# Placing the rows of a mixture of experts: scattered into room per expert, in place of slot lists and gathers

## The chip, the cores and the metric

One of the cores of a Trainium2 chip runs the whole program. The metric is the device time of one execution in microseconds (us). The engines are TensorE (PE in the profile, its weight loads PEld), VectorE (DVE), ScalarE (ACT), GpSimd (POOL) and SyncE (SP). SP and ACT issue plain DMAs; POOL issues the indirect ones, which take their row numbers from a tile in SBUF.

## What is computed

A graph layer of 6250 nodes with 256 features in float32 (100,000 edges), then a mixture of 8 experts, of which each node uses 2. The mixture, cut to what matters:

```python
xt = x.reshape(N, D)                       # 6250 x 256
probs = softmax(xt @ Wr + br)              # 8 experts
top_p, top_idx = top_k(probs, 2)
weights = top_p / top_p.sum(-1, keepdims=True)
xn = (xt - mean) * rsqrt(var + eps)
xe = xn[None] * ln_g[:, None] + ln_b[:, None]
h = gelu(einsum('end,edh->enh', xe, W1) + b1[:, None])     # 256 -> 1024
y = einsum('enh,ehd->end', h, W2) + b2[:, None]            # 1024 -> 256
out = (weights[:, :, None] * take_along_axis(y_tok, top_idx)).sum(1)
x = x + out
```

The kernel computes each expert only for the nodes that chose it, in tiles of 256 (node, choice) pairs.

## The kernel before

NT = 49 tiles of 128 nodes, in G = 7 groups of CT = 7 tiles. P = 128, NP_ = 49 x 128 = 6272 nodes with padding. An expert tile has SLOTS = 256 slots; MT = 56 expert tiles are always computed, which is enough for 12544 pairs wherever they fall. The program has an edge stage (to about 1330 us of the span), a node stage, and the expert stage. All engines run their own instruction stream, written out by hand in order, and meet at semaphores.

**Node stage.** `tensor_nodes`, `vector_nodes`, `scalar_nodes`, `gpsimd_nodes` and `sync_nodes` are one function for each engine. TensorE makes a node tile's last product (second_product, L1452), transposes the node sums (turn, L1461) and multiplies them with the router's weights (logit, L1472), with second_product running 14 tiles ahead. DVE works by group: `scales(g)` writes the normed rows xh (L1588), `measure_rows(g + 2)` adds the products to X (second_sum, L1561) and takes means and variances (L1569 to L1574), `weigh(g - 1)` makes the two weights of each node of the group before (L1623 to L1634), `route(g)` takes logits, the two largest and their indices (L1597 to L1618). ScalarE evicts the transposes (L1767) and takes the exponentials of a group once route has got to s_sm (L1772, L1773). The ring xh has 3 groups; each row is 256 values, 2 weights and 2 expert numbers (DX = 260 words). SP stores X of each group to sum_dram (`summed`) and, once its weights are there, the normed rows to xh_dram in node order (`normed`, L1818).

**After the last group.** DVE compares the chosen experts of all 49 tiles (L1653, L1656), TensorE counts them and ranks them within a tile (L1491, L1492), DVE runs a scan over the tiles for each of the 8 experts (L1662) and makes the table tex of which expert each of the 56 tiles belongs to (L1664 to L1681); this is NODE_EXPERTS, upon which SP begins to load weights. Then each pair has a slot number pos (L1683 to L1695). To turn "node to slot" into "slot to node", for each of the 49 node tiles DVE builds two one-hots from the high and the low part of pos (L1709, L1711), ScalarE scales one by the node number (L1781) and TensorE adds their product up in one PSUM bank (L1499). L1714 to L1722 make of that the slot list slot_i; unused slots point at rows of zeros behind the last node. This is NODE_SLOTS.

**Expert stage.** POOL gathers 128 rows of xh_dram by the slot list, two gathers for each expert tile (`gather`, L2021), two tiles ahead. TensorE transposes them (rows_in, L1881), ScalarE applies the expert's scale and bias (L1983), DVE splits values into a high and a low part (L1924, L1926), TensorE does the up product in three terms (L1896) and the down product (L1909), ScalarE the Gelu between them (L2000). DVE adds the bias and multiplies with the pair's weight (L1965, L1968), and POOL adds the 128 rows into sum_dram by the same slot list (L2039), an indirect DMA with accumulation. SP loads the weights of the tile's expert (`load`, L2043 to L2054). After the last addition sum_dram is copied to the output.

`landed_rows` waits until all normed rows are stored; xh of two groups lies in the region of which the expert stage uses other parts. s_xtra counts the stores of the rows behind the last node.

## Time and profile before

| | us |
|---|---|
| median of 3 timed runs | 2344.48 (2344.31 to 2349.3) |
| the profiled execution | 2321.41 |
| its span, first to last instruction | 2320.0 |

The profile is of one execution. Busy time of each engine over the span, from its page:

| engine | busy us | share |
|---|---|---|
| TensorE, matmuls | 1900.3 | 82% |
| TensorE, weight loads | 1561.9 | 67% |
| DVE | 1658.3 | 71% |
| ScalarE | 1142.4 | 49% |
| POOL | 1279.6 | 55% |

These shares are means over stages with different limits, so the rows below are read by stretch. Other views used: the chain of work that ended last (followed back from the last instruction, at each step to what released it), groups of instructions by line, a timeline in order of time, waits by who waited for whom, and busy time by stretch with the granted TensorE clock (1.00 is full speed). In a row `out<-in` names the tiles, `x49` is a count, and `[1.87 <-PE bank L1492]` is idle time before the instruction and what ended it.

### The profile page before, as it was taken

To read this page: it belongs to the slowest core of one execution; us is meant where nothing else is said; L and a number is where in the kernel's file an instruction comes from. 1 tells how busy PE (TensorE), PEld (TensorE's weight loads), DVE (VectorE), ACT (ScalarE), POOL (GpSimd) and SP (SyncE) were. 2 spreads that over 40 slices of the span, in tenths; PEclk is the share of its full clock that TensorE was granted. 3 is DMA by queue.
4 is the path that set the end of the run, shared out by engine and by line. 5 is a ranking of instruction groups with operands and counts; after the bars stand their busy time and mean duration, and the time that the engine had idled before them with its cause. 6 is when DMAs were issued, how large, how long until landed. Compare 5 with 4: busy or idle time off the path is not lost. (4 is left out here: it accounts for less than half of the span.)

```text
span 2320.0 us, 37945 instructions
## 1 busy us (share of the span) xinstructions
PE 1900.3 (82%) x11157; PEld 1561.9 (67%) x11157; DVE 1658.3 (71%) x5249; ACT 1142.4 (49%) x2281; POOL 1279.6 (55%) x811
## 2 busy tenths in 40 slices
PE   3789996788887978877887277865999999999994
PEld 1466774556665655556666134651999999999994
DVE  4688897687867768673333066768888888888883
ACT  2544442222232332323222114327989988999883
POOL 1467785677778878776777500001355444455542
PEclk7689997898998999998999589865999999999997
DMA  9968875676787787868888663232778888888885
GB/s 319 342 113 159 157 117 101 104 126 113 126 176 112 131 177 123 177 107 197 173 180 167 94 217 114 96 113 92 217 228 237 230 231 238 236 227 231 236 232 161
DMA packets 325848, 401.89 MB, mean 173 GB/s; under 512 B 34983, under 2 KB 267196, under 8 KB 325506
## 3 DMA queue, kind: packets, MB, share of 16 engines
q1 hardware_dynamic: 194048, 257.05, 35.8%
q0 software_dynamic: 103008, 103.83, 32.8%
q10 hardware_dynamic: 28578, 38.50, 5.4%
q8 instruction: 93, 1.52, 0.3%
q14 instruction: 121, 0.99, 0.1%
HBM read 251.13 MB, written 154.55 MB: 175 GB/s over the span
## 5 line engine op out<-in xcount | busy, mean ns | idle before, releaser
L1120 POOL DMA_INDIRECT acc_dram<-third x566 | 917.7, 1621 | 314.0 <-issue 140.0
L2039 POOL DMA_INDIRECT sum_dram<-node,small x112 | 194.7, 1739 | 317.9 <-DVE node L1968 288.8
L1909 PE MATMUL bank<-down_parts 128*128 128x256 f32 x2688 | 335.4, 284 | 0.0
L1896 PE MATMUL bank<-up_parts 128*128 128x256 f32 x2688 | 333.1, 284 | 2.3 <-DVE up_parts L1926 2.3
L1896 PEld LDWEIGHTS bank<-up_parts 128*128 128x128 f32 x2688 | 327.9, 193 | 2.7 <-DVE up_parts L1926 2.7
L1909 PEld LDWEIGHTS bank<-down_parts 128*128 128x128 f32 x2688 | 325.3, 191 | 0.0
L1075 ACT ACTIVATE third<-bank 128x512 f32<-128x512 f32 x283 | 168.7, 597 | 298.7 <-DMA acc_dram<-third 231.8
L555 PE MATMUL bank<-work,third 128*128 128x256 f32 x1132 | 289.9, 398 | 30.9 <-ACT third L1075 27.4
L856 DVE TENSOR_SCALAR third<-fixed,third 128x128 f32<-128x128 f32 x566 | 172.9, 387 | 149.2 <-PE bank L544 149.1
L555 PEld LDWEIGHTS bank<-work,third 128*128 128x128 f32 x1132 | 214.2, 202 | 65.9 <-ACT third L1075 33.1
L2021 POOL DMA_INDIRECT node<-xh_dram,small x112 | 136.1, 1215 | 214.2 <-DVE small L1722 180.4
L1066 ACT ACTIVATE third<-bank 128x512 f32<-128x512 f32 (+1 forms) x142 | 84.7, 597 | 328.4 <-PE bank L544 321.6
L487 PE MATMUL bank<-turned 128*128 128x245 f32 (+2 forms) x432 | 151.4, 448 | 97.6 <-DVE turned L760 80.1
L2000 ACT ACTIVATE node<-bank,node 128x256 f32<-128x256 f32 x448 | 187.8, 471 | 56.4 <-PE bank L1896 56.3
L1953 DVE TENSOR_TENSOR down_parts<-node,down_parts 128x512 fp32r<-128x512 f32 x224 | 155.0, 692 | 65.9 <-ACT down_parts L2006 43.8
L487 PEld LDWEIGHTS bank<-turned 128*128 128x128 f32 x432 | 77.3, 201 | 166.2 <-DVE turned L760 122.3
L544 PEld LDWEIGHTS bank<-third 128*128 128x128 f32 x1132 | 165.3, 215 | 21.2 <-issue 10.4
L544 PE MATMUL bank<-third 128*128 128x128 f32 x1132 | 171.2, 300 | 2.8 <-DVE third L856 2.8
L1916 DVE TENSOR_TENSOR up_parts<-turned,up_parts 128x512 fp32r<-128x512 f32 x224 | 152.9, 684 | 0.3 <-ACT up_parts L1974 0.3
L2006 ACT ACTIVATE down_parts<-node 128x512 fp32r<-128x512 f32 x224 | 141.7, 632 | 7.1
L1916 DVE TENSOR_TENSOR down_parts<-turned,down_parts 128x512 fp32r<-128x512 f32 x224 | 139.8, 686 | 1.8 <-ACT down_parts L1974 0.4
L760 DVE TENSOR_TENSOR turned<-turned,bank 128x245 f32 (+2 forms) x216 | 95.2, 441 | 60.4 <-PE bank L487 52.5
(265 smaller groups left out, 3120.2 us busy)
## 6 DMA issues: line engine op xcount, KB each, us to landing
turned<-in_w_up SPq DMA_DIRECT2D x56, 1024.0 KB, 5.5
turned<-in_w_down SPq DMA_DIRECT2D x56, 1024.0 KB, 11.1
work<-src_dram SPq DMA_DIRECT2D x141, 256.0 KB, 4.2
acc_dram<-fixed SPq DMA_DIRECT2D x15, 1280.0 KB, 10.1
work<-xn_dram SPq DMA_DIRECT2D x146, 128.0 KB, 3.2
work<-acc_dram SPq DMA_DIRECT2D x72, 256.0 KB, 3.4
at_dram<-turned ACTq DMA_DIRECT2D x48, 256.0 KB, 4.2
work<-at_dram ACTq DMA_DIRECT2D x24, 512.0 KB, 4.2
```

The costliest lines, as they stand in the source:

```text
L487: e.matmul(dense_bank(n)[:, 0:HI * s], one_lo[:, t % 4, :], one_hi[:, t % 3, 0:HI * s], start=True, stop=True).then_inc(s_ap, 1)
L544: k = e.matmul(bank[2][:, (t % QUAD) * P:(t % QUAD + 1) * P], OH[:, t % (2 * QUAD), :], S[:, t % (S_QUADS * QUAD), :], start=True, stop=True)
L555: k = e.matmul(bank[3 + h][:, (u - t) * D:(u - t + 1) * D], B[:, u % (2 * QUAD), :], win[:, q % 3, :], start=True, stop=True)
L856: k = e.tensor_scalar(OH[:, t % (2 * QUAD), :], iota_p, dst_rel[:, t:t + 1], w_c[:, t:t + 1], ALU.is_equal, ALU.mult)
L1075: e.activation(M[:, t % (2 * QUAD):t % (2 * QUAD) + 2, :].rearrange("p a b -> p (a b)"), bank[3 + h][:, :], ACT.Copy).then_inc(s_row, 1)
L1120: e.indirect_dma_start(acc_dram[i], bass.IndirectOffsetOnAxis(put_i[:, t:t + 1], 0), M[:, t % (2 * QUAD), :], None, compute_op=ALU.add).th ...
L1896: k = e.matmul(ps, W1s[:, 2 * b + wp, q, h * P:(h + 1) * P], xTs[:, 2 * b + xp, q, :], start=(q == 0 and (wp, xp) == TERMS[0]), stop=(q == ...
L1909: k = e.matmul(bank[5 + c][:, 0:D], hTs[:, hp, h, c * P:(c + 1) * P], W2s[:, 2 * b + wp, h, :], start=(h == 0 and hp == 0 and wp == 0), st ...
L1916: e.tensor_tensor(flat_part(Ws, i, 1, j), flat_raw(W, i, j), flat_part(Ws, i, 0, j).bitcast(F32), ALU.subtract).then_inc(done, 1)
L1953: e.tensor_tensor(two[:, 1], hf[:, j % 2, :], two[:, 0].bitcast(F32), ALU.subtract).then_inc(s_hl, 1)
L2000: e.activation(hf[:, j % 2, (u % 2) * SLOTS:(u % 2 + 1) * SLOTS], bank[1 + j % 4][:, (u % 2) * SLOTS:(u % 2 + 1) * SLOTS], ACT.Gelu, bias= ...
L2039: e.indirect_dma_start(sum_dram, bass.IndirectOffsetOnAxis(slot_i[:, n:n + 1], 0), yb[:, i % 2, c, :], None, compute_op=ALU.add).then_inc( ...
```

## The change

Each expert gets ROOM = 6656 rows in a new tensor xe_dram, enough for all 6272 nodes and one tile more. After route(g), DVE forms the one-hots of the group; TensorE counts them (`count`), DVE gets each pair's row number in its expert's room from a running end for each expert (`places`, in the loop before route(g + 1)), and POOL scatters each node row twice, once for each choice, 14 indirect DMAs a group. The row gets one word more, the node number (DX = 261), so that the expert stage reads from the row where its result is to be added, and no slot list is built. Each expert's used rows end somewhere; from that end on, one tile of unused rows (zeros, with node numbers behind the last node) is stored by ScalarE's queue, 8 such stores whose place is read from a register, and 7 tiles of unused rows behind all rooms. In the expert stage SP loads the 256 rows of a tile by one plain DMA at a row number from the table first_row_i, and POOL only adds. A row goes to partition and half in the same way as before. What is left out below: declarations, the removed lines of lists and slot numbers, and the counts of semaphores that follow.

```diff
-    DX = D + 4
+    DX = D + 5
+    ROOM = -(-NP_ // SLOTS) * SLOTS + SLOTS
+    UNUSED = MT - 2 * NP_ // SLOTS
...
-    xh_dram = nc.dram_tensor("xh_dram", (TRASH + 2 * P, DX), F32, kind="Internal").ap()
+    xe_dram = nc.dram_tensor("xe_dram", (NX * ROOM + UNUSED * SLOTS, DX), F32, kind="Internal").ap()
...
         def landed_rows(e):
 
             for i in range(3):
-                e.wait_ge(s_xhd[i], 16 * len(range(i, G, 3)))
+                e.wait_ge(s_xhd[i], 16 * 2 * CT * len(range(i, G, 3)))
...
+            def count(g):
+
+                e.wait_ge(s_chosen, g + 1)
+                if g >= 2:
+                    e.wait_ge(s_placed, g - 1)
+                chosen = ohs.rearrange("p a b -> p (a b)")
+                e.matmul(bank[4 + g % 2][:, P:P + CT * NX], ones[:, :], chosen, start=True, stop=True)
+                e.matmul(bank[4 + g % 2][:, P + 64:P + 64 + CT * NX], before, chosen, start=True, stop=True).then_inc(s_rank, 1)
+
             for t in range(NT):
                 if t + 2 * CT < NT:
                     second_product(t + 2 * CT)
                 turn(t)
                 if t:
                     logit(t - 1)
+                if t >= CT and t % CT == 4:
+                    count(t // CT - 1)
             logit(NT - 1)
...
-            for t in range(NT):
-                s = t % 4
-                e.wait_ge(s_hot, 2 * t + 2)
-                e.wait_ge(s_hota, t + 1)
-                for i in range(2):
-                    k = e.matmul(bank[7][:, 0:2 * LISTS], hot_lo[:, s, i, :], hot_hi[:, s, i].rearrange("p v n -> p (v n)"),
-                                 start=(t == 0 and i == 0), stop=(t == NT - 1 and i == 1))
-                k.then_inc(s_list, 1)
+            count(G - 1)
...
                 if g >= 3:
-                    e.wait_ge(s_xhd[g % 3], 16 * (g // 3))
+                    e.wait_ge(s_xhd[g % 3], 16 * 2 * CT * (g // 3))
                 e.tensor_copy(xh[g % 3][:, :, D + 2:D + 4], topi[:, a:b, 0:2])
+                e.tensor_copy(xh[g % 3][:, :, D + 4].bitcast(I32), token[:, a:b])
                 e.tensor_copy(idf[:, a:b], topi[:, a:b, 0:2]).then_inc(s_idf, 1)
+                e.wait_ge(s_idf, g + 1)
+                vec.done(e.tensor_tensor(oh, iota8.unsqueeze(1).unsqueeze(1).broadcast_to((P, 2, CT, NX)),
+                                         idf[:, a:b].rearrange("p t i -> p i t").unsqueeze(3).broadcast_to((P, 2, CT, NX)),
+                                         ALU.is_equal))
+                vec.wait()
+                e.tensor_tensor(ohs, oh[:, 0], oh[:, 1], ALU.add).then_inc(s_chosen, 1)
+
+            def places(g):
...
+                ends = incl[:, (g - 1) % 2, :, CT - 1] if g else room_at
+                e.wait_ge(s_rank, g + 1)
+                vec.wait()
+                vec.done(e.tensor_copy(counted, by_expert(P)))
+                vec.wait()
+                vec.done(e.tensor_tensor_scan(flat(incl[:, g % 2]), flat(more), flat(counted), 0.0, ALU.mult, ALU.add))
+                vec.wait()
+                vec.done(e.tensor_tensor(incl[:, g % 2], incl[:, g % 2], ends.unsqueeze(2).broadcast_to((P, NX, CT)), ALU.add))
+                vec.wait()
+                vec.done(e.tensor_tensor(place, incl[:, g % 2], counted, ALU.subtract))
+                vec.wait()
+                e.tensor_tensor(place, place, by_expert(P + 64), ALU.add).then_inc(s_placed, 1)
+                e.wait_ge(s_placed, g + 1)
+                vec.done(e.tensor_tensor(oh_place, oh, place.rearrange("p x t -> p t x").unsqueeze(1).broadcast_to((P, 2, CT, NX)),
+                                         ALU.mult))
+                vec.wait()
+                vec.done(e.tensor_reduce(posf, oh_place, AX.X, ALU.add))
+                vec.wait()
+                e.tensor_copy(pos_i[:, a:b].rearrange("p t i -> p i t"), posf).then_inc(s_pos, 1)
...
                 if g:
                     weigh(g - 1)
+                    places(g - 1)
                 route(g)
...
+            for i in range(UNUSED):
+                unused_rows(slice(NX * ROOM + i * SLOTS, NX * ROOM + (i + 1) * SLOTS))
+            e.wait_ge(s_once, NODE_EXPERTS)
+            for x_ in range(NX):
+                at = e.value_load(room_end[0:1, x_:x_ + 1], min_val=0, max_val=NX * ROOM)
+                unused_rows(bass.ds(at, SLOTS))
...
+            for g in range(G):
+                e.wait_ge(s_pos, g + 1)
+                e.wait_ge(s_wgt, g + 1)
+                e.wait_ge(s_xh, g + 1)
+                e.wait_ge(s_idf, g + 1)
+                for t in group(g):
+                    for i in range(2):
+                        e.indirect_dma_start(xe_dram, bass.IndirectOffsetOnAxis(pos_i[:, t, i:i + 1], 0), xh[g % 3][:, t - g * CT, :],
+                                             None).then_inc(s_xhd[g % 3], 16)
...
+                e.tensor_copy(slot_i[:, 2 * i:2 * i + 2], xe[:, i % 3, :, D + 4].bitcast(I32)).then_inc(s_wr, 1)
...
+            def rows(i):
+                if i >= 3:
+                    e.wait_ge(s_xeT, i - 2)
+                    e.wait_ge(s_wr, 3 * (i - 2))
+                at = e.value_load(first_row_i[0:1, i:i + 1], min_val=0, max_val=NX * ROOM + (UNUSED - 1) * SLOTS)
+                e.dma_start(xe[:, i % 3], xe_dram[bass.ds(at, SLOTS), :].rearrange("(c p) d -> p c d", p=P)).then_inc(s_xe[i % 3], 16)
+
             e.wait_ge(s_once, NODE_EXPERTS)
             e.wait_ge(s_sumd, 16 * G)
             e.wait_ge(s_xh, G)
+            weights(0)
+            weights(1)
             landed_rows(e)
-            for i in range(MT):
-                load(i)
+            e.wait_ge(s_xtra, XTRA)
+            for i in range(3):
+                rows(i)
+            for i in range(2, MT):
+                weights(i)
+                if i + 1 < MT:
+                    rows(i + 1)
```

## Rows read from the trace of the kernel before

**Rows 1.** chain that ended last, expert stage starts: start us, us

```profile
1614.22 3.23 DMA node<-xh_dram,small
...
1620.99 7.30 PE bank L1896 x48
```

**Rows 2.** the same chain, last expert tile

```profile
2273.23 0.44 PE bank L1881 x4
...
2279.41 5.76 PE bank L1896 x48
2285.17 5.77 PE bank L1909 x48
```

**Rows 3.** groups by line, from 1620: busy us, mean ns, idle

```profile
L1896 PE MATMUL bank<-up_parts 128*128 128x256 f32 x2688 | 333.1, 284 | 2.3 <-DVE up_parts L1926 2.3
```

**Rows 4.** the same chain in the routing groups

```profile
1480.14 0.58 DVE small L1574 x7
...
1530.88 0.58 DVE small L1574 x7
...
1559.04 1.05 DVE work L1653 x2
```

**Rows 5.** timeline, start of the last two routings

```profile
1544.36 0.22 DVE L1597 TENSOR_TENSOR work<-work,small 128x56 f32<-128x56 f32 x1 [4.89 <-PE bank L1472]
...
1555.86 0.22 DVE L1597 TENSOR_TENSOR work<-work,small 128x56 f32<-128x56 f32 x1 [4.57 <-PE bank L1472]
```

**Rows 6.** line L1781: ns min/median/max, first and last start

```profile
L1781 ACT ACTIVATE work<-work x98: 465/467/482, 1574.1 to 1610.2; 128x224 bf16<-128x224 bf16 x98
```

**Rows 7.** scatter-add L1120 and gather L2021, each line's view

```profile
L1120 POOL DMA_INDIRECT acc_dram<-third x566: 1559/1561/7581, 95.6 to 1315.7; - x189
...
DMA to landing us min/median/max: 3.7/4.2/8.2
...
L2021 POOL DMA_INDIRECT node<-xh_dram,small x112: 949/1117/1439, 1612.9 to 2265.4; - x112
```

**Rows 8.** timeline, from the experts' table to SP's first load

```profile
1567.23 0.62 DVE L1677 TENSOR_REDUCE small<-work 128x56 f32<-128x448 f32 x1
...
1568.11 0.19 DVE L1681 CAST small<-small 128x56 int32<-128x56 f32 x1
...
1569.11 0.40 SPq L2051 DMA_DIRECT2D turned<-in_w_up  x1
```

**Rows 9.** groups by line, DVE, 1430 to 1562 us

```profile
L1602 DVE TENSOR_TENSOR work<-work,small 128x56 f32<-128x56 f32 x7 | 1.5, 217 | 0.2
```

**Rows 10.** timeline, second and third group: start us, us, engine

```profile
1480.63 0.18 DVE L1623 TENSOR_REDUCE work<-work 128x7 f32<-128x56 f32 x1
...
1485.18 2.35 DVE L1588 TENSOR_SCALAR work<-node,small,work 128x256 f32<-128x256 f32 x7
...
1497.38 0.51 PE L1472 MATMUL bank<-work 128*128 128x8 f32 x4
1497.44 0.18 DVE L1623 TENSOR_REDUCE work<-work 128x7 f32<-128x56 f32 x1
...
1498.62 0.21 DVE L1597 TENSOR_TENSOR work<-work,small 128x56 f32<-128x56 f32 x1
```

**Rows 11.** timeline of POOL, an early gather and one in mid stage

```profile
1614.22 1.44 POOL L2021 DMA_INDIRECT node<-xh_dram,small  x1 [0.31 <-issue]
...
1917.55 1.12 POOL L2021 DMA_INDIRECT node<-xh_dram,small  x1 [0.30 <-issue]
```

**Rows 12.** the page, DMA issues: KB, us to landing

```profile
work<-acc_dram SPq DMA_DIRECT2D x72, 256.0 KB, 3.4
```

**Rows 13.** waits of SP's queue: us, times, longest

```profile
SPq L2049 <- DVE node L1968: 473.3, 53, 10.8
```

**Rows 14.** busy PE, PEld, DVE, ACT, POOL; PEclk, DMA, GB/s

```profile
1519.00:1536.00 17.00, 12.04 (x62) 10.32 (x62) 12.04 (x66) 5.87 (x14) 0.00 (x0) 0.80 0.33 110
1536.00:1548.00 12.00, 8.58 (x42) 8.18 (x42) 6.70 (x45) 3.00 (x11) 0.00 (x0) 0.50 0.27 93
```

More of the change, by code:

```diff
@@ L1351, in gps_layer @@
         topi = work(NT, 8, dtype=U32)
-        oh1 = work(NT, NX)
-        oh2 = work(NT, NX)
-        ohs = work(NT, NX)
-        place = work(NT, NX)
-        cnt = work(NT, NX)
         prob = work(NT, 2)
@@ L1359, in gps_layer @@
         idf = work(NT, 2)
-        posf = work(NT, 2)
         pos_i = work(NT, 2, dtype=I32)
-        pos_b = work(NT, 2, dtype=I32)
-        pos_hi = work(NT, 2)
-        pos_lo = work(NT, 2)
         token = work(NT, dtype=I32)
-        token_b = work(NT, dtype=I32)
-        token_hi = work(NT)
-        token_lo = work(NT)
+        oh = work(2, CT, NX)
+        oh_place = work(2, CT, NX)
+        ohs = work(CT, NX)
+        counted = work(NX, CT)
+        incl = work(2, NX * CT).rearrange("p a (x t) -> p a x t", x=NX)
+        place = work(NX, CT)
+        posf = work(2, CT)
+        more = work(NX, CT)
+        room_at = work(NX)
+        room_end = work(NX, dtype=I32)
+        gap = work(NX)
+        first_row = work(MT)
+        unused_id = work(2, dtype=I32)
+        unused = work(2, DX)
         tot = work(NX)
@@ L1648, in vector_nodes @@
                     weigh(g - 1)
+                    places(g - 1)
                 route(g)
-            e.wait_ge(s_idf, G)
-            for i, oh in enumerate((oh1, oh2)):
-                vec.done(e.tensor_tensor(oh, iota8.unsqueeze(1).broadcast_to((P, NT, NX)),
-                                         idf[:, :, i:i + 1].broadcast_to((P, NT, NX)), ALU.is_equal))
-            vec.wait()
-            e.tensor_tensor(ohs, oh1, oh2, ALU.add).then_inc(s_once, 1)
-            weigh(G - 1)
-            e.wait_ge(s_rank, 1)
-            vec.done(e.tensor_copy(cnt.rearrange("p a b -> p (a b)"), bank[0][:, 0:NT * NX]))
-            vec.wait()
-            for x_ in range(NX):
-                vec.done(e.tensor_tensor_scan(place[:, :, x_], ones[:, 0:NT], cnt[:, :, x_], 0.0, ALU.mult, ALU.add))
-            vec.wait()
-            vec.done(e.tensor_scalar(toti, place[:, NT - 1, :], float(SLOTS - 1), None, ALU.add))
+            weigh(G - 1)
+            places(G - 1)
+            ends = incl[:, (G - 1) % 2, :, CT - 1]
+            vec.done(e.tensor_copy(room_end, ends))
+            vec.done(e.tensor_tensor(tot, ends, room_at, ALU.subtract))
+            vec.wait()
+            vec.done(e.tensor_scalar(toti, tot, float(SLOTS - 1), None, ALU.add))
             vec.wait()
@@ L1670, in vector_nodes @@
             vec.done(e.tensor_tensor_scan(endf, ones[:, 0:NX], tot, 0.0, ALU.mult, ALU.add))
+            vec.done(e.tensor_scalar(gap, tot, -1.0, float(ROOM), ALU.mult, ALU.add))
             vec.wait()
-            e.wait_ge(s_tst, 2)
             vec.done(e.tensor_tensor(tcmp, tile_start.unsqueeze(2).broadcast_to((P, MT, NX)),
@@ L1679, in vector_nodes @@
             vec.done(e.tensor_scalar(tex, tex, float(NX - 1), None, ALU.min))
+            vec.done(e.tensor_tensor(tcmp, tcmp, gap.unsqueeze(1).broadcast_to((P, MT, NX)), ALU.mult))
             vec.wait()
-            e.tensor_copy(tex_i, tex).then_inc(s_once, 1)
-            vec.done(e.tensor_tensor(base, endf, tot, ALU.subtract))
-            vec.done(e.tensor_tensor(place, place, cnt, ALU.subtract))
+            vec.done(e.tensor_copy(tex_i, tex))
+            vec.done(e.tensor_reduce(first_row, tcmp, AX.X, ALU.add))
@@ L1685, in vector_nodes @@
             vec.wait()
-            vec.done(e.tensor_tensor(place, place, bank[1][:, 0:NT * NX].rearrange("p (a b) -> p a b", b=NX), ALU.add))
+            vec.done(e.tensor_tensor(first_row, first_row, tile_start, ALU.add))
             vec.wait()
-            vec.done(e.tensor_tensor(place, place, base.unsqueeze(1).broadcast_to((P, NT, NX)), ALU.add))
-            for i, oh in enumerate((oh1, oh2)):
-                vec.wait()
-                vec.done(e.tensor_tensor(ohs, oh, place, ALU.mult))
-                vec.wait()
-                vec.done(e.tensor_reduce(posf[:, :, i], ohs, AX.X, ALU.add))
@@ L1713, in vector_nodes @@
-            e.wait_ge(s_list, NT)
-            vec.done(e.tensor_scalar(slot_f, bank[7][:, 0:LISTS], 64.0, float(TRASH), ALU.mult, ALU.add))
-            vec.wait()
-            vec.done(e.tensor_tensor(slot_f, slot_f, bank[7][:, LISTS:2 * LISTS], ALU.add))
-            vec.wait()
-            e.wait_ge(s_tst, 3)
-            vec.done(e.scalar_tensor_tensor(out=slot_t, in0=slot_f, scalar=float(TRASH), in1=slot_pad.rearrange("p a b -> p (a b)"),
-                                            op0=ALU.is_equal, op1=ALU.mult))
@@ L1721, in vector_nodes @@
[L1721 to L1722 removed]
+            e.tensor_copy(first_row_i, first_row).then_inc(s_once, 1)
         def scalar_nodes(e):
@@ L1943, in vector_experts @@
             rows_in(0)
+            landed_rows(e)
+            e.wait_ge(s_xtra, XTRA)
             for j in range(4):
@@ L2042, in sync_experts, with weights @@
         def sync_experts(e):
-            def load(i):
+            def weights(i):
                 b = i % 2
```

120 lines of the change are left out of this document (27 added, 93 removed).

## The prediction

> **What bounds the kernel now.** I read the busy table of the page, then the chain of work that ended last, then stretches of it. The expert stage is settled first: from its first matmul at 1620.99 us [rows 1] to the last, ended at 2290.94 us, TensorE runs tile after tile, up product, transposes, down product [rows 2]. 5.76 + 0.44 + 5.77 = 11.97 us a tile, times 56 is 670 us, against 1620.99 to 2290.94 = 669.95 us. Its up products waited there for 2.3 us in all, once, for DVE's split of the first rows [rows 3]; no gather of POOL's after the first stopped it. So the expert stage can't get shorter by this change; it can only start earlier or later. Everything hangs on when TensorE starts it: 1620.99 us.
>
> What sets that start: the routing of seven groups, 16.9 us apart for the first five (1480.14 to 1530.88 is three of them, [rows 4]) and then 11.5 us [rows 5]; then, after the last routing ends at 1559.04 [rows 4], the ranks and the slot lists. The 98 scaled one-hots of L1781 alone run from 1574.1 to 1610.7 [rows 6]. Then gather, landing, transposes, bias, split, up to 1620.99 [rows 1]. From 1559.0 to 1620.99 is 62 us of tail, in which POOL does nothing until its first gather at 1612.9 [rows 7].
>
> **What goes.** The tail's two big rank matmuls, eight scans over 49 tiles, the 98 compares, the 98 scalings, 98 list matmuls, the list's arithmetic and the first two gathers. Most of it lies between the experts' table at 1568.30 [rows 8], which stays, and the first gather at 1612.9: taken alone it would bring TensorE's start some 44.6 us forward. The plain load of xh_dram rows by SP also goes.
>
> **What comes, on DVE and TensorE, group by group.** After route(g): a token copy, the comparison of 112 elements and the sum of 56. The nearest row is a DVE op of 56 elements at 217 ns [rows 9]; with the gap to the next, where each waits for the last, I take 0.25, a little less for 7 elements and 0.32 for 112: 0.16 + 0.32 + 0.25, about 0.7 us. It stands behind the s_sm increments, so ScalarE's exponentials go on, but ahead of scales(g+1) and the second sums, whose PSUM banks TensorE needs: I count 0.6 us for each of groups 0 to 4. places(g-1) is eight such ops, two of them on 112 elements: 2.2 us, ahead of route(g). TensorE's last logits of the group are done at 1497.89 when route(1) starts at 1498.62 [rows 10], so 0.7 us of it is covered: net 1.5 us, in iterations 1 to 4. In iterations 5 and 6 DVE now waits 4.6 to 4.9 us for the logits [rows 5], and that covers places. count(g) is two TensorE matmuls with weight loads, and I give it the 0.51 us of a group of four narrow ones of L1472 [rows 10], on TensorE, which paces the tiles. So a group takes 16.9 + 0.6 + 1.5 + 0.5 = 19.5 us in place of 16.9. After the last group, weigh, count and places, then twelve DVE ops, three of them on 448 elements (0.62 us each, [rows 8]): about 4.5 us.
>
> Positions ready, P(g): weigh(0) began at 1480.63, takes 1.2 us (the next one is 1497.44 to 1498.62, [rows 10]), shifts by 0.6, then 2.2: P(0) = 1484.6. P(1) = 1504.1, P(2) = 1523.6, P(3) = 1543.1; P(4) about 1556, P(5) 1568, P(6) 1575; the experts' table at 1580.
>
> **What comes, on POOL.** 98 indirect scatters of 128 rows of 1044 bytes, 14 a group, and this is the term that decides. Before shows no plain scatter. Two neighbours: the gather of 1040-byte rows takes 949 ns at least, 1117 in the median, and the scatter-add of 1024-byte rows 1559 ns at least and 1561 in the median (L1120) [rows 7], each with 0.30 us of issue before the next [rows 11]. A gather is one row read and one row written, as a plain scatter is; the scatter-add reads the destination as well. I therefore lean on the gather: with POOL alone 0.95 + 0.30 = 1.25, in the expert stage, beside a busy DVE, 1.12 + 0.30 = 1.42 [rows 11]. I take 1.40 us; the ends are 1.25 and 1.86, both above nothing because POOL has to issue each.
>
> At 1.40 a group needs 19.6 us, just what the routing then takes, so POOL runs without a gap from 1484.9: the last of 98 starts at 1484.9 + 97 x 1.40 = 1620.7. The tail freed of lists is thus filled by scatters, since groups 4 to 6 come at 12 us each and POOL needs 19.6. Their landing: L1120's writes take 3.7 us at least and 4.2 in the median from issue [rows 7]: 1624.9.
>
> Behind it on SP: landed_rows, the xtra wait and three row loads, with weights(2) queued behind them (not wanted before tile 2). From release to first issue 0.8 us (the experts' table is written at 1568.30, SP's first DMA goes out at 1569.11, [rows 8]); a load of 256 KB lands in 3.4 us [rows 12]: 1629.1. From landing to the first matmul 1617.45 to 1620.99, 3.5 us [rows 1]: TensorE starts at 1632.6, 11.6 us later than before. weights(0) and (1) are issued at 1581 and are there long before. The scratch rows written by ACT (15 x 267 KB) start at 1580 and are hidden by the scatters; if ACT's last were late, it would add its own 4 us. Buffers: scales(4), (5), (6) now wait for scatters(1), (2), (3), due at 1527, 1547 and 1566; they come at about the same times, so they cost the routing up to 6 us, which POOL's backlog covers. A copy of the slot number (0.16 us a tile) on DVE and a row load in SP's queue, with more than one tile of slack [rows 13], are hidden in the expert stage by TensorE.
>
> A rule that speaks against the change: the gather that lay beside a DVE subtraction took 1.44 us [rows 11] where the least is 0.95, yet 566 scatter-adds beside a busy DVE have median 1561 and minimum 1559, so no stretching shows there [rows 7]. The Trainium skill, SBUF — State Buffer, "SBUF: two separate sides", says that DVE, running a two-port mode, locks GpSimd out of the port through which it writes descriptors, and that the ACT or SP queue is immune. By that rule the seven scaled rows of L1588 (2.35 us in a group, [rows 10]) would each hold POOL up; L1120's rows disagree, the gather's 1.44 agrees.
>
> **Sum.** The profiled execution's span is 2320.0 us (2321.41 with what lies around it); 11.6 more gives 2331.6. The median of the timed runs is 2344.48, 23.1 above the profiled time; this stands apart from the change and I carry it over: 2344.5 + 11.6 = 2356.1 us.
>
> **Rivals.**
> 1. POOL at the gather's floor, 1.25 us. Group g takes 17.5 us, so POOL waits for P(3) = 1543.1, then does 56: last start 1543.1 + 55 x 1.25 = 1611.9, plus 4.2 + 0.8 + 3.4 + 3.5: start 1623.8, +2.8 us, 2347.3. No measurable difference. For it: the gathers' least, 949 ns [rows 7]. Chance 0.17.
> 2. The other side, faster: a scatter costs less than any gather seen, or the routing is delayed less. The point is 1543.1 + 55c + 11.9 = 1621.0, c = 1.20 us; if P(3) came 4 us earlier, c = 1.27. At c = 1.05 the start is 1612.8: -8.2, 2336.3. For it: 62 us of tail is a large reserve, and landing may be nearer to the first gather's 3.2 us [rows 1]. Against: no row under 0.95 + 0.30. Chance 0.18.
> 3. The scatter has the scatter-add's price, or DVE stretches each as the 1.44 us gather: 1.74 to 1.86 us. Last start 1484.9 + 97 x 1.86 = 1665.3, start 1677.2, +56 us, 2400.7; at 1.74, +44.6, 2389. For it: both write into DRAM by a list of offsets. Against: one descriptor less a row. Chance 0.16. With only the 2.35 us a group of L1588 as a hold-up, in five groups, it would be +11.8 on top of the forecast, 2368: chance 0.07.
> 4. The edit doesn't do what it says, because the expert stage then waits for row loads: SP issues rows(i+1) behind weights(i), which waits for DVE's L1968. SP waited 473.3 us of the stage's 670 for that line, at most 10.8 at a time [rows 13]: its own work is short and it stays more than a tile ahead; no chance of weight.
>
> **Chances.** The forecast (c 1.30 to 1.55, +5 to +22) has 0.42, own range 2349 to 2366. Rival 3 with its hold-up form 0.23: slower 0.65. Same 0.17, faster 0.18 (a measurement of this kernel can tell about 0.2%, 4.7 us, from no change). To leave out no more than 2 in 10 the range reaches from 2338, within the faster case, to 2400.
>
> **What would show each step.** POOL's scatters: their median duration and whether POOL has gaps before 1560; L1574 to L1574 about 19.5 us; the first expert matmul near 1632 with SP's row load waiting on DMA, the expert stage 669.9 us long as before. I am wrong if the scatter's duration is outside 1.0 to 1.25 us, if TensorE's granted clock, 0.80 in the fifth group and 0.50 after 1536 [rows 14], falls to half earlier and the groups take over 22 us, or if the expert stage itself changes length.

## The result, and the profile after

| | before | after |
|---|---|---|
| median of four timed runs, us | 2344.39 (2343.58 to 2349.3) | 2378.97 (2374.33 to 2384.76) |
| the profiled execution | 2321.41 | 2374.33 |
| its span | 2320.0 | 2372.9 |

The changed kernel takes 1.0164 times as long (95% interval 1.012 to 1.0208), 34.6 us by the medians. The forecast was 11.6 us. The two profiled executions are 52.9 us apart. The first scaled rows (DVE's first instruction on a group's normed rows) start at 1453.6 us of the span before and at 1452.8 after, so up to there these two traces take the same time. Where kernels are compared below, times are given from this point on ("+114.5" is 114.5 us behind it), because the point itself moves from execution to execution (last section).

| from the first scaled rows, us | before | after |
|---|---|---|
| the experts' table | +114.5 | +177.5 |
| first expert matmul | +167.4 | +219.3 |
| end of the span | 866.4 | 920.1 |

The expert stage did not change: from its first matmul to TensorE's last it takes 669.9 us before and 671.8 after. In the chain that ended last (start us, us, what) the last tile of after reads as [rows 2] did:

```profile
2332.48 5.76 PE bank L1875 x48
2338.24 5.77 PE bank L1888 x48
```

So 52 of the 53.7 us at the end are there when TensorE begins it. The experts' table came 63.0 us late, and the shorter tail (41.9 us from table to matmul, where it was 52.9) gave 11 of that back.

The line view of the scatters (ns min/median/max, first and last start, what ended the idle time before them) gives the term on which the prediction hung, the price of a scatter:

```profile
L1781 POOL DMA_INDIRECT xe_dram<-turned,work x70: 968/972/1099, 1488.2 to 1653.5; - x70
L1781 POOL DMA_INDIRECT xe_dram<-work x28: 968/972/1098, 1541.6 to 1635.6; - x28
its engine sat idle before it (us, times) until:
  DVE work L1643: 98.1, 5
  issue: 28.6, 93
```

0.972 us and 0.30 of issue: 1.275 us a scatter, near the gathers' least [rows 7]. POOL waited 98.1 us, in five waits, for positions. So POOL was not the bound of the routing groups; the routing itself was. The starts of DVE's routing (first L1600 of each group) are 24.4, 26.1, 27.3, 26.0, 40.2 and 12.3 us apart, where L1607 of before has 15.9, 16.8, 16.9, 17.0, 11.8 and 11.5.

Why, the timeline shows (start us, us, engine, line; in brackets the idle time and what ended it). This is inside the first run of 14 scatters, 1488.23 to 1505.9:

```profile
1498.90 0.38 PE L1458 MATMUL bank<-fixed,node 128*128 128x128 f32 x2
...
1500.88 0.38 PE L1458 MATMUL bank<-fixed,node 128*128 128x128 f32 x2
...
1502.62 0.42 DVE L1554 TENSOR_TENSOR node<-node,bank 128x256 f32<-128x256 f32 x1 [4.34 <-remote]
...
1504.74 0.38 ACT L1752 ACTIVATE work<-bank 128x256 f32<-128x256 f32 x1 [6.07 <-remote]
```

TensorE had finished the transposes at 1499.28 and 1501.26; ACT evicts them from 1504.74 on. "Remote" is the profile's word for an end of waiting that it can put down to no instruction of this core's engines. Between 1440 and 1690 us before has no such wait. In the run of 28 scatters, 1567.58 to 1603.4, it is worse:

```profile
1577.64 0.38 ACT L1752 ACTIVATE work<-bank 128x256 f32<-128x256 f32 x1 [3.58 <-PE bank L1458]
1584.77 0.38 ACT L1752 ACTIVATE work<-bank 128x256 f32<-128x256 f32 x1 [6.75 <-remote]
1594.68 0.38 ACT L1752 ACTIVATE work<-bank 128x256 f32<-128x256 f32 x1 [9.53 <-remote]
```

```profile
1583.35 0.22 DVE L1628 COPY work<-bank 128x56 f32<-128x56 f32 x1 [8.54 <-remote]
...
1595.11 1.03 PE L1469 MATMUL bank<-work 128*128 128x8 f32 x4 [8.37 <-ACT work L1752]
...
1607.36 0.22 DVE L1590 TENSOR_TENSOR work<-work,small 128x56 f32<-128x56 f32 x1 [21.83 <-remote]
```

DVE stood for 21.83 us and went on 4 us after the run was over. The logits that it waits for, TensorE's L1469, were done at 1596.14; so 10.6 us of the gap are a wait for TensorE, which was itself held up through ACT, and 11.2 us passed with the input complete. Summed over 1440 to 1690 us, "remote" gaps ahead of ACT and DVE instructions are 89.0 us. That is idle time which ended late, not all of it time with the input ready, and gaps of the two engines overlap; it serves to compare kernels, not to be added up to the loss. The prediction had no term for it.

### The profile page after: what moved, and what is told of

It reads as the page before. It is cut to its first block and busy times, and to the rows that moved or that the text cites. A ratio compares the mean times of both kernels' runs of the same rounds, so it can differ in the third digit from the quotient of the medians.

```text
span 2372.9 us, 37978 instructions
## 1 busy us (share of the span) xinstructions
PE 1901.6 (80%) x11059; PEld 1579.1 (67%) x11083; DVE 1633.8 (69%) x5262; ACT 1106.6 (47%) x2183; POOL 1230.7 (52%) x797
## 5 line engine op out<-in xcount | busy, mean ns | idle before, releaser
L1954 ACT ACTIVATE up_parts<-turned 128x512 fp32r<-128x512 f32 x224 | 122.5, 623 | 38.0 <-issue 37.2
```

## The experiments

Kernels whose names begin with b are the kernel before with something added; those with a are the changed kernel with something altered. Only a_mix is timed in rounds; the others are one profiled execution each, read from their traces. There is one trace of each kernel, so how far the distances from the first scaled rows move between executions of one kernel isn't known; b_sp, below, gives before's back to 0.1 us at the table and 1.3 at the first matmul. "Remote" is summed over ACT and DVE from 1440 to 1690 us throughout; some traces (of after, but also of b_sp, which has no gap in that window) also have 16 to 21 us of it in the edge stage, 2.9 us at most at a time, which is left out. Executions of before beside them took 2347.8 us (first four), 2344.03 (next four) and 2336.79 (median of 13, last four).

**The scatters by themselves, and everything but them.** b_scat leaves before as it is and adds 98 plain scatters to spare tables, at the places where the changed kernel has them:

```diff
+                for t in group(g):
+                    for i in range(2):
+                        e.indirect_dma_start(scr_dram[i], bass.IndirectOffsetOnAxis(token[:, t:t + 1], 0), xh[g % 3][:, t - g * CT, :],
+                                             None).then_inc(s_scr[g % 3], 16)
```

Two kinds of added waits are left out here and in the kernels made from b_scat: those for the group's rows, ahead of the loop, and those that keep a group of the ring xh until its DMAs have landed.

> The kernel before, with POOL scattering each group's 14 x 128 rows (two copies, to scratch tensors nobody reads, rows in node order) as soon as the weights of the group are there; nothing else is added but the wait that keeps the ring of normed rows. Theory 1 (a dense run of scatters holds up ScalarE and DVE while their inputs are ready): the routing, 1453 to 1559 us before, gets 25 to 45 us longer, with idle gaps of 3 to 20 us at the evictions of the transposes, at the second sums and at the first op of route, inside the scatter runs; span 2345 to 2370. Theory 2 (the gaps come from the new counts and places, not from the scatters): routing and span within 6 us of the kernel before.

Measured 2400.69 us, span 2399.2; from the first scaled rows the table is at +170.1, the first expert matmul at +232.0, the end 64.9 us later than before's. The line of the transposes' eviction:

```profile
L1772 ACT ACTIVATE work<-bank x49: 361/383/385, 1467.8 to 1624.1; 128x256 f32<-128x256 f32 x49
its engine sat idle before it (us, times) until:
  PE bank L1464: 42.6, 22
  remote: 37.1, 6
```

"Remote" gaps sum to 102.1 us. The scatters' addition alone brings the stalls into a kernel that had none, and costs more than the 25 to 45 us that I expected. The longest gap shows again how much of one is time with the input complete: the logits were done at 1598.53, so 14.6 of its 29.14 us.

```profile
1597.51 1.02 PE L1475 MATMUL bank<-work 128*128 128x8 f32 x4 [4.09 <-issue]
...
1613.17 0.22 DVE L1601 TENSOR_TENSOR work<-work,small 128x56 f32<-128x56 f32 x1 [29.14 <-remote]
```

a_noscat is the changed kernel without scatters. It stores the normed rows plainly, in node order, and the expert stage reads them in that order and adds its results to spare rows, so the experts' input and the output are not the reference's; choose, count and places stay.

```diff
-                        e.indirect_dma_start(xe_dram, bass.IndirectOffsetOnAxis(pos_i[:, t, i:i + 1], 0), xh[g % 3][:, t - g * CT, :],
-                                             None).then_inc(s_xhd[g % 3], 16)
...
+                e.dma_start(xh_dram[g * CT * P:(g + 1) * CT * P, :].rearrange("(t p) d -> p t d", p=P),
+                            xh[g % 3]).then_inc(s_xhd[g % 3], 16)
```

> The changed kernel without the scatters: SP stores the normed rows of a group with one plain DMA, the expert stage loads 256 rows in node order at a fixed place by the same plain load, and adds all results to spare rows; counts, places, row numbers and the stores of unused rows stay. Left out: the scatters and so the right rows. Theory 1: no gap over 5 us in the routing, the seven groups take some 105 + 18 us, the experts' table comes at about 1583 and the first expert matmul 35 us behind it at about 1618 (the stores of unused rows and the first weights still share the DMA engines); span about 2317. Theory 2: the gaps of 6 to 22 us stay and the table comes near 1631 as in the changed kernel, span about 2360.

Measured 2323.41, span 2321.9: no "remote" gap, table at +132.8, matmul at +161.7, end 4.9 us earlier than before's. So in this execution choose, count and places came with a table 18.3 us later, and without scatters the shorter tail (28.9 us, where before has 52.9) more than pays for it. The 18.3 us aren't theirs alone: the groups are 18.4, 19.7, 24.4, 24.3, 12.7 and 12.3 us apart, and the two of 24.4 and 24.3 ran at a granted clock of 0.51 and 0.57. Had they taken 19.7 like the one before them, the table would have come 9.3 us earlier. By that estimate the change could give about 14 us without the scatters' cost; measured are 4.9.

**Gaps between the scatters.** a_space:

```diff
+                        e.iota(idle_t, [[1, P]], base=0, channel_multiplier=0, allow_small_or_imprecise_dtypes=True).then_inc(s_idle, 1)
+                        idles += 1
+                        e.wait_ge(s_idle, idles)
                         e.indirect_dma_start(xe_dram, bass.IndirectOffsetOnAxis(pos_i[:, t, i:i + 1], 0), xh[g % 3][:, t - g * CT, :],
...
```

> The changed kernel with an iota of 128 columns and a wait for it ahead of each scatter, so that a scatter comes every 1.6 to 1.8 us in place of 1.275. Theory 1 in the form 'it is the rate': the gaps in the routing shrink to less than half of the changed kernel's (there about 60 us in all), and the last scatter starts at 1488 + 97 x 1.7 = 1653 or a little later, span 2365 to 2375. If it is the time that a run of scatters lasts and not its rate, the gaps grow with the longer runs and the span goes over 2385. Theory 2: the gaps are what they are without spacing, 2373 to 2380.

POOL's timeline shows the spacing:

```profile
1602.93 0.25 POOL L1784 IOTA work<- 128x128 f32 x1
1603.46 0.98 POOL L1787 DMA_INDIRECT xe_dram<-turned,work  x1 [0.28 <-POOL work L1784]
1604.47 0.25 POOL L1784 IOTA work<- 128x128 f32 x1
1605.00 0.99 POOL L1787 DMA_INDIRECT xe_dram<-turned,work  x1 [0.28 <-POOL work L1784]
```

A scatter starts every 1.54 us in place of 1.275, takes as long as it did (0.98), and no "remote" gap is left. 2369.78 us; table +143.1, matmul +199.2. With a slower POOL the kernel was 20.1 us faster from the first scaled rows on (900.0 against 920.1), by one trace of each. Now POOL is the last engine of the stage (last scatter at about 1658, matmul at 1667.6).

**The unused rows' stores.** a_early issues the seven stores of whole unused tiles, whose places are fixed, ahead of ACT's loop.

```diff
+            e.wait_ge(s_unused, 1)
+            for i in range(UNUSED):
+                unused_rows(slice(NX * ROOM + i * SLOTS, NX * ROOM + (i + 1) * SLOTS))
             for g in range(G):
```

> The changed kernel with the seven stores of unused rows at fixed places issued by ScalarE's queue ahead of the routing loop, not after it. They are 1.87 MB; behind the last group the DMA engines moved 8 MB of unused rows, weights and scatters in about 36 us. Theory of the tail (DMA bound from the last group to the first row load): first row load 5 to 6 us earlier than in the changed kernel, 2367. Rival (the eight register loads and stores on ScalarE's queue are slow in themselves, 3.5 us each): 4 us earlier by the issue time alone, since the eight start when the table is there, and no more. If neither, no difference.

2393.32 us, where 2367 was expected; "remote" 79.6 us, table +188.4. The stores stand in ACT's queue from 1462.79 to 1466.97, ahead of the first eviction of transposes, which comes 3.3 us behind the first scaled rows and in after 0.2 us before them. The granted clock is 0.55 from 1466 to 1485, where after has 1.00 at this place (1453 to 1463.4). The first routing begins 21.8 us behind the first scaled rows in place of 10.7, which makes up the 10.9 us by which the table is later than after's. That wait for the queue is a part of it and the clock the rest; whether the stores brought the clock down isn't shown. From table to matmul are 39.1 us where after has 41.9. So the seven stores take 3 us of the tail. The other eight, which need the counts, are the longer part. In the trace of after (ACT's and SP's queues, and then the chain) they take 27.89 us to issue:

```profile
1632.27 27.89 ACTq L1725 DMA_DIRECT2D xe_dram<-work  x8
```

```profile
1632.57 0.70 SPq L2016 DMA_DIRECT2D turned<-in_w_up  x1
1635.39 0.70 SPq L2017 DMA_DIRECT2D node<-in_cols_expert  x1
```

```profile
1659.82 5.28 DMA xe_dram<-work
1665.89 2.82 DMA node<-xe_dram
1668.75 1.13 PE bank L1861 x4
1671.42 0.70 DVE up_parts L1905
1672.17 2.93 PE bank L1875 x12
```

In a_noscat the same eight take 10.80 us:

```profile
1595.17 10.80 ACTq L1726 DMA_DIRECT2D xe_dram<-work  x8
```

From 1634 to 1658 us, inside and just behind the last run of 28 scatters (1619.05 to 1654.5), ACT's and SP's queues go forward by turns, one instruction in about 0.70 us. Even register operations are caught. Line view of after, then of a_noscat:

```profile
L1725 ACTq FUSED_REGOPS  x8: 19/45/699, 1632.1 to 1659.7; - x8
```

```profile
L1726 ACTq FUSED_REGOPS  x8: 42/42/48, 1595.0 to 1605.5; - x8
```

The medians are alike, but two of the eight, at 1646.7 and 1655.1, took 691 and 699 ns, where the longest of a_noscat took 48. This instruction computes on registers. What a long run of scatters holds up is therefore not only signals between engines.

**Bytes, direction, alignment, or the way of issue.** Four versions of b_scat. b_sp writes the same 98 x 128 rows by plain DMAs of SP's queue:

```diff
-                        e.indirect_dma_start(scr_dram[i], bass.IndirectOffsetOnAxis(token[:, t:t + 1], 0), xh[g % 3][:, t - g * CT, :],
-                                             None).then_inc(s_scr[g % 3], 16)
...
+                        e.dma_start(scr_dram[i][t * P:(t + 1) * P, :], xh[g % 3][:, t - g * CT, :]).then_inc(s_scr[g % 3], 16)
```

> The kernel before, with the same 98 rows-tiles per the whole routing as the added scatters carried (14 stores of 129 KB a group, to the same two spare tables in DRAM), but as plain stores on SP's queue and none on POOL's. The bytes into DRAM, the buffers that they hold (xh of three groups) and the place in the loop stay. Theory A (the scatters' way of being issued, one row for each partition's index from POOL, is what holds up ACT and DVE): no idle time of ACT's zT line and DVE's second_sum line put down to 'remote' beyond 3 us in sum; the experts' table within 5 us of the kernel before's own distance from the first scales (+114.5), about 2348 to 2353 us in all. Rival B (the bytes or the writes in DRAM hold them up): the stalls come back, 30 us or more in sum, and about 2375 to 2400 us.

b_gath gathers rows of 1024 bytes out of DRAM in place of writing them. It also waits, ahead of each group, until the gathers of the group before have landed, so its runs are all of 14, where b_scat has three of 14 and two of 28:

```diff
+                if g:
+                    e.wait_ge(s_scr[(g - 1) % 3], 16 * 2 * CT * ((g - 1) // 3 + 1))
...
-                        e.indirect_dma_start(scr_dram[i], bass.IndirectOffsetOnAxis(token[:, t:t + 1], 0), xh[g % 3][:, t - g * CT, :],
-                                             None).then_inc(s_scr[g % 3], 16)
+                        e.indirect_dma_start(W2.rearrange("p a k n -> p (a k) n")[:, 2 * (t - g * CT) + i, :], None, xn_dram,
+                                             bass.IndirectOffsetOnAxis(token[:, t:t + 1], 0)).then_inc(s_scr[g % 3], 16)
```

> The kernel before, with 98 gathers of 128 rows of 1024 bytes (out of the rows' table in DRAM into a stretch of SBUF that nothing reads) on POOL in the place of the 98 added scatters, in the same runs of 14 a group. The direction is turned round, the way of issue is kept; nothing is written into DRAM by them. Theory A (POOL's making of a descriptor for every row, with its writes of them): the stalls of ACT and DVE put down to 'remote' stay, 25 us or more in sum, and about 2375 to 2400 us. Rival B (writes into DRAM, many small ones): the stalls are gone, under 5 us in sum, and at most 2356 us.

b_quart carries 256 bytes of each row, and b_align 1024 bytes at a pitch of 1024 (`D` where b_quart has `D // 4`); the source is cut to the same width:

```diff
-    scr_dram = [nc.dram_tensor(f"scr{i}_dram", (TRASH, DX), F32, kind="Internal").ap() for i in range(2)]
+    scr_dram = [nc.dram_tensor(f"scr{i}_dram", (TRASH, D // 4), F32, kind="Internal").ap() for i in range(2)]
```

> The kernel before, with the 98 added scatters carrying 256 bytes a row in place of 1044: the same number of instructions and rows, a quarter of the bytes. Theory A: stalls as with the full rows, about 94 us of 'remote' in sum down to 60 at the least, and 2385 to 2401 us. Rival B (bytes): a quarter of the stalls or none, and at most 2362 us. What a scatter occupies POOL for should stay at 0.95 to 1.0 us by A, since a descriptor is made for each row whatever its length.

> The kernel before, with the 98 added scatters carrying rows of 1024 bytes at a pitch of 1024 in place of 1044 at 1044: every row begins at a multiple of 1024 bytes, and no row is cut. Rival C (rows that straddle, so that a write must first read what stands beside it) gives at most half of the 94 us of 'remote' and at most 2375 us. Theory A gives no change: 2390 to 2402 us.

| | us | "remote", ACT and DVE, us | table | first matmul |
|---|---|---|---|---|
| b_scat | 2400.69 | 102.1 | +170.1 | +232.0 |
| b_sp | 2332.7 | 0 | +114.5 | +168.7 |
| b_gath | 2387.89 | 107.4 | +179.3 | +232.1 |
| b_quart | 2401.55 | 85.9 | +166.9 | +229.3 |
| b_align | 2394.36 | 81.2 | +171.7 | +233.8 |

b_sp's groups are 15.9, 16.8, 16.9, 17.0, 11.8 and 11.5 us apart, the intervals of before to the tenth, while its DMA engines were far busier (columns: busy us of PE, PEld, DVE, ACT, POOL, then clock, DMA share, GB/s), with 222 GB/s where b_quart stalls at 81:

```profile
1507.00:1524.00 17.00, 13.66 (x70) 11.81 (x70) 12.10 (x67) 5.95 (x14) 0.00 (x0) 0.80 0.75 222
```

```profile
1524.00:1550.00 26.00, 20.19 (x75) 16.32 (x74) 12.27 (x67) 5.63 (x13) 13.24 (x14) 0.61 0.25 81
```

Neither the bytes, nor writing, nor the alignment, nor the number of DMAs that report to a semaphore (14 a group in each) makes the difference. What is left is the way of issue: indirect DMAs of 128 rows from POOL against plain ones from SP. No run has plain DMAs from POOL, so which half of that it is, the engine or the list of rows, isn't shown.

Part of the distance between these tables isn't the stalls' own. In b_scat the first interval between groups, which ends ahead of its first scatter, is 21.6 us long at a clock of 0.61, where b_sp has 15.9. In b_quart it is 15.9 as in before, and its table is 52.4 us late all the same.

**How long a run without a pause may be.** a_half has a_space's pause ahead of every second scatter (`if i:` before it), a_four ahead of every fourth (`if i and t % 2:`), and b_seven is b_scat with one scatter a tile, so in runs of seven:

```diff
-                    for i in range(2):
+                    for i in range(1):
```

> The changed kernel, with the pause of the spaced version (a small iota on POOL and the wait for it, about 0.27 us) ahead of every second scatter in place of every one: a scatter each 1.275 and 1.54 us in turn, mean 1.41. Theory A1 (a pause of POOL lets the held-up signals through, however often it comes): idle time put down to 'remote' under 5 us in sum, as in the spaced version; the experts' table 143 to 148 us behind the first scales; POOL is still the last engine of the stage, so the first expert matmul comes about 193 us behind the first scales (spaced: +199.2) and the whole about 2364 us. Theory A2 (the mean rate counts, with its bound between 1.275 and 1.41 us): as A1. Theory A3 (its bound lies between 1.41 and 1.54 us): over 30 us of 'remote', the table at +160 or later, about 2375 us or more.

> The changed kernel, with that pause ahead of every fourth scatter (mean 1.34 us; a run without a pause is 4 to 6 scatters, 5 to 7.6 us). Theory A1 (the stalls build up over 8 us and more of a run without a pause, and a pause clears them): under 15 us of 'remote' in sum, and about 2362 us. Theory A2 or A3 (mean rate): if the half-spaced version stalls, this one stalls more (over 50 us); if it doesn't, this one may lie on either side.

> The kernel before with 49 added scatters in place of 98: one for a tile, in runs of 7 (8.9 us) without a pause, then POOL idle for the rest of the group's 17 us or so. Theory A1 (stalls come only from 8 to 12 us into a run on): under 15 us of 'remote' in sum and at most 2354 us. Rival (every scatter costs the others its share, at whatever place in the run): half of what 98 scatters cost, so about 47 us of 'remote' and about 2372 us.

| mean period of scatters | kernel | "remote", us | table | first matmul | end of span |
|---|---|---|---|---|---|
| 1.275 us | after | 89.0 | +177.5 | +219.3 | 920.1 |
| 1.34 | a_four | 61.2 | +163.9 | +203.5 | 903.4 |
| 1.41 | a_half | 29.4 | +161.7 | +198.2 | 897.5 |
| 1.54 | a_space | 0 | +143.1 | +199.2 | 900.0 |
| 1.275 in runs of 7 | b_seven | 4.6 | +123.4 | +176.3 | 875.7 |

The whole times are 2350.74 (a_four), 2365.42 (a_half) and 2337.24 us (b_seven). A1, that a pause clears the hold-up however often it comes, falls: 61.2 and 29.4 us where under 15 and under 5 were expected. So does A2. A3, a bound of the mean period between 1.41 and 1.54 us, comes near for a_half ("remote" 29.4 where over 30 was expected, table +161.7 where +160 or later) and holds for a_four (over 50). But the pace inside a run doesn't decide alone: b_seven has the full pace in runs of 8.8 us and all but no gap, where its rival form gave 47 us. What fits all five is a backlog that grows while POOL issues at full pace and drains when it pauses; no row shows the backlog itself. For the whole time the three spacings come out alike (897.5 to 903.4 from the first scaled rows): what the table gains by longer pauses, the last scatter loses. b_seven's only gap lies where two of its runs joined to 14 (1538.21 to 1555.8), and it ends at 1555.20:

```profile
  PE bank L1464: 45.2, 30
  issue: 8.8, 3
  remote: 4.6, 1
```

The table is 8.9 us later than before's all the same, and nearly all of it belongs to that joined run: its groups are 17.2, 17.1, 17.1, 17.1, 20.3 and 11.5 us apart.

**The three findings put together.** a_mix has the pauses in the first five groups and none in the last two. The seven stores of a_early stand ahead of ACT's loop too, but earlier than there: before the two `norm_roots` that come ahead of it, where they don't hold up the first evictions.

```diff
+                        if g < G - 2:
+                            e.iota(idle_t, [[1, P]], base=0, channel_multiplier=0, allow_small_or_imprecise_dtypes=True).then_inc(s_idle, 1)
+                            idles += 1
+                            e.wait_ge(s_idle, idles)
...
```

> The changed kernel as well as these findings let me put it: a pause ahead of each scatter in the first five groups, while ACT and DVE still route; none in the last two, since POOL is then the last engine of the stage; and the seven unused tiles' stores with fixed places ahead of the loop. By my theory the experts' table stays about 143 us behind the first scales and the last scatter starts 28 times 0.27 us (7.6 us) earlier than in the spaced version, so the first expert matmul comes at about +190 (spaced +199, changed +219, before +167), and the whole at about 2361 us, between the kernel before (2344) and the changed one (2379). The rival, that the 28 scatters at full pace hold up the last of the routing again, gives +205 and about 2375 us.

Median of 10 runs 2348.55 (2341.81 to 2356.25), before 2336.79 (median of 13): ratio 1.0048, interval 1.0019 to 1.0078. It takes back about two thirds of the loss, more than I expected (2361), but doesn't beat before. No "remote" gap; table +135.9, matmul +184.4. POOL now works almost without a wait, and DVE waits for it:

```profile
L1788 POOL DMA_INDIRECT xe_dram<-turned,work x70: 969/988/1155, 1487.9 to 1631.2; - x70
L1788 POOL DMA_INDIRECT xe_dram<-work x28: 968/980/1082, 1531.6 to 1613.3; - x28
its engine sat idle before it (us, times) until:
  POOL work L1785: 19.4, 70
  issue: 8.5, 28
who waited for it (us, times):
  DVE turned L1583: 11.4, 2
```

From 1487.9 to 1632.2 is 144.3 us for 98 scatters, 1.47 each, and that is the bound that is left: the stage can't end before POOL has issued the scatters of 12544 rows. The last 28, at full pace from 1596.7, held up no routing, since the table was out at 1592.33. The eight stores took 12.5 us to issue (1594.6 to 1607.1), with the scatters' first 10 us at full pace beside them; SP's steps of 0.70 us are there at 1634.46, just behind the 28. Here too the hold-up comes late in a run and outlasts it.

That a_mix beat its forecast of +190 goes with a difference in TensorE's granted clock. The rows are the third group of a_noscat, the third of a_space and the third of a_mix (columns as above):

```profile
1510.00:1534.00 24.00, 21.10 (x73) 18.09 (x74) 14.12 (x75) 5.88 (x13) 0.00 (x0) 0.51 0.23 78
```

```profile
1524.00:1548.00 24.00, 21.18 (x74) 18.11 (x74) 14.09 (x76) 5.87 (x13) 19.01 (x31) 0.52 0.36 125
```

```profile
1508.00:1529.00 21.00, 15.13 (x74) 13.13 (x74) 14.98 (x79) 5.88 (x13) 16.83 (x28) 0.76 0.39 134
```

With the same matmuls a group takes 24.4 us at 0.51 (1.2 GHz) and 20.5 at 0.76, scatters or not. After starts with such a group, ahead of its first scatter: 1464 to 1488 at a clock of 0.56, 24.4 us. Before still held 0.80 in its fifth group [rows 14]. I made no run that varies the clock alone, so what makes a group fall to the lower level is open; that it costs about 4 us a group is read from these rows.

## Why the prediction was right in sign and short in size

1. **Expert stage, unchanged: right.** Its up products waited 2.3 us in after as in [rows 3], and the stage takes 671.8 us where it took 669.9. Rival 4, row loads that come late, did not show.
2. **The price of a scatter: nearly right.** 1.40 us was taken, 1.25 was an end, 1.275 is measured. Rival 3 (1.74 and more) fell, and the gather was the right neighbour. With 1.275 and all else as I had it, the sum would have been rival 1's, about +4 us.
3. **"POOL runs without a gap from 1484.9": wrong.** P(0) came at 1488.2, and POOL then waited 98.1 us in all. The chain went through the routing.
4. **The group of 19.5 us is the term that was mis-sized.** Choose and places were well costed: L1628 to L1643 took 2.2 us (1511.84 to 1514.02), and a_noscat's second interval is 19.7 us. But in after the intervals are 26 to 27 us and once 40.2. I had priced a scatter by what it costs POOL and by nothing that it costs the others. b_scat against b_sp gives the price of that omission: 55.6 us at the table (52.4 between b_quart and b_sp). In after the table is 44.7 us later than in a_noscat. Each of these numbers holds the stalls and the difference in granted clock between the two executions; no run parts them.
5. **The clock.** The condition "falls to half earlier and the groups take over 22 us" was named as what would make me wrong. It came true in after's first group and in two groups of a_noscat. It belonged into the sum, with a chance, since it goes with about 4 us a group.
6. **"Hidden by the scatters" for the stores of unused rows: wrong.** The last landed at 1665.10, 10.6 us after the last scatter's end at 1654.5, where a scatter's landing would have given about 4 [rows 7]. In a_noscat they alone hold the tail: 10.80 us of issue and 7.60 of landing.
7. **"If ACT's last were late, 4 us": too small,** because the queue's own issue had slowed to 3.5 us a store.
8. **The 23.1 us between the profiled time and the median, carried over: wrong.** In after the two are 4.6 us apart. Before's profiled execution was its fastest (2321.41; 13 later ones are 2326.14 to 2348.9, median 2336.79, which would make the change 42.2 us). A term-by-term sum on that trace belongs to the 52.9 us between the profiles, so its +11.6 missed by 41 us where the medians show 23.

So the sign was right by luck: I expected POOL to be late, and the routing was, held up by POOL. That the measured time lies in the wide range is luck too. It is above the forecast's own 2349 to 2366 and below rival 3's 2389 to 2401, and no branch of the prediction held what happened.

Rival 3 named hold-ups of POOL by DVE (the Trainium skill, SBUF — State Buffer, "SBUF: two separate sides"). The trace shows none of that: scatters beside a busy DVE have median 972 ns and maximum 1099. No row tells whether DVE's instructions here ran in the mode that the section speaks of. The gather of 1.44 us was a weak sign from the start: the one ahead of it, beside the same DVE line, L1916, took 1.03. The reverse took place, DVE and ACT held up beside POOL.

## What to carry to other kernels

Price an indirect DMA twice: by what POOL pays, and by what a run of them without a pause costs the other engines. Here 14 in a row at 1.275 us held up ACT and DVE, runs of 7 hardly did, and a pause of 0.27 us ahead of each took the stalls away, so slower issue gave a faster kernel. Look also at what stands behind new work in an engine's queue: seven stores put ahead of the first evictions held these up for 3.5 us and saved 3 in the tail. When a step moves from a stretch where one engine works alone into one where four do, look first for what they share; and ask of a change that deletes 45 us of tail which engine is then last, since the freed time goes to that one.

## What was not expected of the hardware

- Beside runs of 14 or more indirect DMAs at full pace, ACT and DVE stand idle for up to 29 us at a time, of which up to 14.6 us with their inputs complete, whatever the bytes (256 to 1044 a row) and the direction. In after's last run, and for 3.4 us beyond its end, ACT's and SP's queues go forward in steps of 0.70 us, and a register operation took up to 699 ns where 48 is the most without scatters. Of after's 13 gaps, 7 end 1 to 4 us behind the end of a run (run to 1532.0, gap to 1532.91; run to 1603.4, gap to 1607.36).
- The same bytes as plain DMAs of SP, at 222 GB/s, cost the routing nothing (its six intervals are before's).
- Scatters of 256-byte and of 1044-byte rows occupy POOL alike: medians 969 ns both (b_quart, b_scat). A plain scatter costs 0.97 + 0.30 us, a scatter-add 1.56 + 0.30 [rows 7].
- The first scaled rows start between 1445.8 (a_four) and 1469.8 us (b_quart) in kernels whose work up to there is all but the same. A spread of 24 us lies ahead of the changed stage, as large as most effects here.
- What stays open: by what way POOL's indirect DMAs reach the other engines' sequencers, whether plain DMAs issued by POOL would do it too, and what makes the clock fall in one execution's group and not in another's.
